# Sorted edge rows placed so that the four rows a partition gets of a unit lie side by side, in a graph network on one core

## The reference

```python
edge_index = jnp.stack([src, dst])        # 206250 edges, sorted by dst, 6250 nodes
x = _layernorm(x + _L0_gnn_ref(x, edge_index, ...))
x = _layernorm(x + _L1_gnn_ref(x, edge_index, edge_attr_64, ...))

# _L0: two layers of   agg = segment_mean(h[src], dst);  relu(agg @ W_l + b_l + h @ W_r)
# _L1:
row, col = (edge_index[0], edge_index[1])
out = jnp.concatenate([x[row], edge_attr], axis=1)
out = jax.nn.selu(out @ W1a + b1a) @ W1b + b1b
summed = jax.ops.segment_sum(out, col, num_segments=x.shape[0])
mean = summed / jnp.maximum(counts, 1.0)[:, None]
h = jnp.concatenate([x, mean, u[batch]], axis=1)
return jax.nn.selu(h @ W2a + b2a) @ W2b + b2b
```

## Time and profile before

| | |
|---|---|
| median of 3 runs | 3544.66 us (3544.01 to 3555.59) |
| the profiled execution | 3541.63 us, span of its instructions 3539.9 us |
| busy share of the span | PE 67%, PEld 48%, DVE 44%, ACT 28%, POOL 51% |
| mean granted TensorE clock | 0.782 of full |
| DMA traffic | 346.58 MB in 478137 packets, 357799 of them under 512 bytes |

### The profile page before, as it was taken

The page is one execution under the profiler, slowest core; times in us unless marked ns, Lnnn a source line. Parts: engine busy times, 40 slices in busy tenths (PEclk is TensorE's granted clock), DMA queues, the critical chain, the costliest instruction groups (busy, mean ns, idle before and its releaser), DMA issues.

```text
span 3539.9 us, 52139 instructions
## 1 busy us (share of the span) xinstructions
PE 2367.1 (67%) x18396; PEld 1684.3 (48%) x18396; DVE 1560.6 (44%) x3112; ACT 989.8 (28%) x2190; POOL 1805.8 (51%) x1857
## 2 busy tenths in 40 slices
PE   2799999887888872465666656565665666564554
PEld 1455555444444432354545545454554554453553
DVE  6689999343443332233433333333333333342333
ACT  3567777100000012122222222222222222221222
POOL 6345555454555547445454544455454444545552
PEclk9999999898989975677777777777777767776556
DMA  6467777659555512322222222222222221221111
GB/s 225 154 186 212 211 249 227 177 171 192 174 175 174 175 40 67 79 43 47 46 47 48 47 43 46 46 45 48 46 48 48 45 44 42 47 46 41 42 38 35
DMA packets 478137, 346.58 MB, mean 98 GB/s; under 512 B 357799, under 2 KB 428536, under 8 KB 474219
## 3 DMA queue, kind: packets, MB, share of 16 engines
q1 hardware_dynamic: 367281, 272.49, 26.9%
q0 software_dynamic: 54368, 57.36, 7.1%
q10 hardware_dynamic: 56250, 13.52, 1.9%
HBM read 200.71 MB, written 142.39 MB: 97 GB/s over the span
## 4 chain that ended last, share of the span: by engine, by line
PE 31%; another core or an unknown queue 25%; issue 20%; DVE 13%; ACT 4%; DMA 3%; SPq 2%; POOL 2%; DVEq 1%; ACTq 0%; POOLq 0%
PE agg_ps L1481 6%; DVE arena L1804 5%; PE u_ps L1612 4%; PE cnt_ps L1573 3%; PE u_ps L1608 2%; PE agg_ps L1622 2%; PE cnt_ps L1352 2%; PE agg_ps L1581 1%; PE v_ps L1598 1%; PE t_ps L1565 1%; PE agg_ps L1359 1%; PE agg_ps L1358 1%; DMA overlapping_rows<-A_sb 1%; DVEq L2121 1%
## 5 line engine op out<-in xcount | busy, mean ns | idle before, releaser
L954 POOL DMA_INDIRECT A_sb<-source_terms,src_cur x1176 | 1120.3, 953 | 1047.9 <-ACT src_cur L1160 707.7
L907 POOL DMA_INDIRECT sorted_edges<-pm_row,pm_to x440 | 480.1, 1091 | 332.2 <-DVE pm_to L1913 208.3
L1612 PE MATMUL u_ps<-arena 128*128 128x64 bf16 x3399 | 252.1, 213 | 355.7 <-issue 354.2
L1481 PE MATMUL agg_ps<-A_sb,arena 128*128 128x448 f16 x1911 | 419.3, 369 | 69.2 <-issue 66.5
L1804 DVE TENSOR_TENSOR arena<-iota_code,arena 128x2048 f16<-128x2048 f16 (+1 forms) x392 | 435.6, 1180 | 38.1 <-PE cnt_ps L1352 36.2
L1049 ACT ACTIVATE A_sb<-cnt_ps 128x392 f32 (+1 forms) x784 | 386.2, 497 | 168.8 <-PE cnt_ps L1352 115.0
L1612 PEld LDWEIGHTS u_ps<-arena 128*128 128x128 bf16 x3399 | 198.5, 111 | 411.5 <-issue 403.0
L2123 DVE TENSOR_TENSOR A_sb<-A_sb,agg_ps 65x48 f32 (+1 forms) x290 | 78.0, 269 | 710.4 <-remote 525.2
L1352 PE MATMUL cnt_ps<-arena 128*128 128x98 f16 x3136 | 283.7, 214 | 54.0 <-DVE arena L1804 23.2
L1481 PEld LDWEIGHTS agg_ps<-A_sb,arena 128*128 128x128 bf16 x1911 | 188.8, 101 | 269.9 <-issue 127.6
L1352 PEld LDWEIGHTS cnt_ps<-arena 128*128 128x128 f16 x3136 | 191.1, 101 | 243.4 <-issue 173.6
(11 more groups left out here) (300 smaller groups left out, 3379.9 us busy)
## 6 DMA issues: line engine op xcount, KB each, us to landing
counts_matrix<-A_sb SPq DMA_DIRECT2D x14, 5488.0 KB, 17.2
A_sb<-counts_matrix SPq DMA_DIRECT2D x12, 5488.0 KB
arena<-in_edge_attr_dram SPq DMA_DIRECT2D x96, 256.0 KB
sorted_edges<-zrow SPq DMA_DIRECT2D x11, 1716.0 KB
A_sb<-source_terms,src_cur POOLq DMA_INDIRECT x1176
arena<-sorted_edges SPq DMA_DIRECT2D x143, 128.0 KB
overlapping_rows<-A_sb SPq DMA_DIRECT2D x1, 13056.0 KB, 39.5
A_sb<-in_edge_attr_dram SPq DMA_DIRECT2D x50, 256.0 KB
```

Source lines behind the costliest of these rows:

```text
L907: pool.indirect_dma_start(out=sorted_d, out_offset=bass.IndirectOffsetOnAxis(ap=pm_to[:, k, j:j + 1], axis=0), in_=pm_row[:, k, j, :], in_ ...
L954: pool.indirect_dma_start(out=gath[k][:, j * F:(j + 1) * F], out_offset=None, in_=p_d, in_offset=bass.IndirectOffsetOnAxis(ap=src_cur[k][: ...
L1481: ins = pe.matmul(agg_ps[:, 0:SBN], Hsb[:, part, blk, :], Asb(half)[:, blk, :], start=False, stop=(part == 2), skip_group_check=True)
L1612: ins = pe.matmul(u_ps[:, j * F:(j + 1) * F], lane_p[u % 2][:, a, j * P:(j + 1) * P], P3[:, 2 * b + a, part, :], start=False, stop=(part = ...
```

## The change

A row's place in `sorted_d` is changed inside its unit. Before, the row with place 128 t + p of a unit (tile t, partition p) lay at 128 t + p; now it lies at 4 p + t. The four rows of a partition are then one piece of 1056 bytes. `slot_group` works out the new number with five more small DVE operations. `load_unit` is one transfer of 128 pieces into `rows_p`. `turn_unit` becomes 4 transposes of 66 columns, one per tile, so that row 64 of `t2_ps` holds the lanes of all 512 edges; `move_unit` copies 64x512 and 1x512; `spread_lanes` is one product of a single row (`pick` row of ones) with 512 columns; `unit_product` does the attribute part tile by tile, with 64 rows of contraction and the 64x64 weights. The ring of `attrT_p` has 2 buffers in place of 3.

```diff
@@ buffers
-        endsT = [edge_buf(P // 2, 2 * UT).bitcast(BF16) for _ in range(2)]
+        endsT = [edge_buf(UT * P // 2, F + 1).bitcast(BF16)[F:F + 1, :] for _ in range(2)]
+        attrT_p = [edge_buf(UT * P, F)]
...
-        attr_p = [edge_buf1(UT * F) for _ in range(UNIT_RING)]
-        ends_p = [edge_buf1(2 * UT) for _ in range(UNIT_RING)]
-        attrT_p = [edge_buf1(UT * F) for _ in range(UNIT_RING)]
+        rows_p = [edge_buf1(UT * (F + 2)).rearrange("p (j f) -> p j f", j=UT) for _ in range(UNIT_RING)]
...
-        pick = sb("pick", [2 * UT, UT, P], BF16)
+        pick = sb("pick", [F + 1, P], BF16)
@@ load_unit
-                sp.dma_start(attr_p[k].rearrange("p (j f) -> p j f", f=F), rows_u[:, :, 0:F]).then_inc(unit_in[k], 16)
-                sp.dma_start(ends_p[k].rearrange("p (j a) -> p j a", a=2), rows_u[:, :, F:F + 2]).then_inc(unit_in[k], 16)
+                sp.dma_start(rows_p[k].rearrange("p j f -> p (j f)"),
+                             sorted_d[u * UT * P:(u + 1) * UT * P, :].rearrange("(p j) f -> p (j f)", p=P)).then_inc(unit_in[k], 16)
@@ move_unit
-                if u >= UNIT_RING:
-                    act.wait_ge(unit_z, UNIT_Z + u - UNIT_RING + 1)
                 if u >= 2:
+                    act.wait_ge(unit_z, UNIT_Z + u - 1)
                     act.wait_ge(lanes_spread, LANES_SPREAD + u - 1)
-                act.activation(attrT_p[u % UNIT_RING], t2_ps[:, 0:UT * F], ACT.Copy)
-                act.activation(endsT[u % 2], t2_ps[0:2 * UT, UT * F:UT * F + P], ACT.Copy).then_inc(unit_moved, 1)
+                act.activation(attrT_p[u % 2], t2_ps[0:F, :], ACT.Copy)
+                act.activation(endsT[u % 2], t2_ps[F:F + 1, :], ACT.Copy).then_inc(unit_moved, 1)
@@ turn_unit
-                for c in range(UT // 2):
-                    pe.transpose(t2_ps[:, c * P:(c + 1) * P], attr_p[k][:, c * P:(c + 1) * P], ident[:, :])
-                pe.transpose(t2_ps[0:2 * UT, UT * F:UT * F + P], ends_p[k], ident[:, :]).then_inc(unit_turned, 1)
+                for j in range(UT):
+                    ins = pe.transpose(t2_ps[0:F + 2, j * P:(j + 1) * P], rows_p[k][:, j, :], ident[:, :])
+                ins.then_inc(unit_turned, 1)
@@ spread_lanes
-                for j in range(UT):
-                    ins = pe.matmul(v_ps[:, j * P:(j + 1) * P], pick[:, j, :], endsT[u % 2], start=True, stop=True)
-                ins.then_inc(lanes_spread, 1)
+                pe.matmul(v_ps[:, :], pick[F:F + 1, :], endsT[u % 2], start=True, stop=True).then_inc(lanes_spread, 1)
@@ unit_product
-                    c = j // 2
-                    if j % 2 == 0:
-                        pe.matmul(u_ps[:, c * P:(c + 1) * P], attrT_p[u % UNIT_RING][:, c * P:(c + 1) * P], Wedge[:, :], start=True, stop=False, skip_group_check=True)
+                    pe.matmul(u_ps[:, j * F:(j + 1) * F], attrT_p[u % 2][:, j * P:(j + 1) * P], Wedge[0:F, 0:F], start=True, stop=False, skip_group_check=True)
@@ slot_group
-                dve.scalar_tensor_tensor(pm_to[:, k, :], pm_rank[:, :], -1.0, pm_else[:, :], ALU.add, ALU.add).then_inc(pm_rows, 1)
+                step(dve.scalar_tensor_tensor(pm_place[:, :], pm_rank[:, :], -1.0, pm_else[:, :], ALU.add, ALU.add))
+                dve.tensor_scalar(pm_lane[:, :], pm_place[:, :], P - 1, None, ALU.bitwise_and).then_inc(dve0, 1)
+                n0[0] += 1
+                step(dve.tensor_scalar(pm_tile[:, :], pm_place[:, :], 7, None, ALU.arith_shift_right))
+                step(dve.tensor_scalar(pm_tile[:, :], pm_tile[:, :], UT - 1, None, ALU.bitwise_and))
+                step(dve.scalar_tensor_tensor(pm_part[:, :], pm_lane[:, :], float(UT - 1), pm_place[:, :], ALU.mult, ALU.add))
+                dve.scalar_tensor_tensor(pm_to[:, k, :], pm_tile[:, :], -float(P - 1), pm_part[:, :], ALU.mult, ALU.add).then_inc(pm_rows, 1)
```

More of the change, by code:

```diff
@@ L328, in build @@
         at1[0] = p_at
-        attr_p = [edge_buf1(UT * F) for _ in range(UNIT_RING)]
-        ends_p = [edge_buf1(2 * UT) for _ in range(UNIT_RING)]
-        attrT_p = [edge_buf1(UT * F) for _ in range(UNIT_RING)]
+        rows_p = [edge_buf1(UT * (F + 2)).rearrange("p (j f) -> p j f", j=UT) for _ in range(UNIT_RING)]
         lane_p = [edge_buf1(2 * UT * P // 2).bitcast(BF16).rearrange("p (a n) -> p a n", a=2) for _ in range(2)]
         hot_p = [edge_buf1(UT * PWIN).rearrange("p (j n) -> p j n", j=UT)]
+        attrT_p.append(edge_buf1(UT * P, F))
+        at1[0] = max(at1[0], p_at + SRC_BLOCKS * F)
         iota_p = edge_buf1(PWIN)
@@ L353, in build @@
         pm_to = sb("pm_to", [P, PRING, EJ], I32)
+        pm_place, pm_lane, pm_tile, pm_part = (sb(n, [P, EJ], I32) for n in ("pm_place", "pm_lane", "pm_tile", "pm_part"))
         pm_seen = sb("pm_seen", [P, 2, NCELL], FP16)
@@ L743, in load_unit @@
             def load_unit(u):
-                k, rows_u = u % UNIT_RING, sorted_d[u * UT * P:(u + 1) * UT * P, :].rearrange("(j p) f -> p j f", p=P)
+                k = u % UNIT_RING
                 if u >= UNIT_RING:
                     sp.wait_ge(lanes_hot, LANES_HOT + u - UNIT_RING + 1)
-                sp.dma_start(attr_p[k].rearrange("p (j f) -> p j f", f=F), rows_u[:, :, 0:F]).then_inc(unit_in[k], 16)
-                sp.dma_start(ends_p[k].rearrange("p (j a) -> p j a", a=2), rows_u[:, :, F:F + 2]).then_inc(unit_in[k], 16)
+                sp.dma_start(rows_p[k].rearrange("p j f -> p (j f)"),
+                             sorted_d[u * UT * P:(u + 1) * UT * P, :].rearrange("(p j) f -> p (j f)", p=P)).then_inc(unit_in[k], 16)
             te = gE * EG
@@ L884, in _ @@
             pool.memset(pm_keep[:, :, :], 1.0).then_inc(pm_const, 1)
-            pool.memset(pick[:, :, :], 0.0).then_inc(pm_const, 1)
+            pool.memset(pick[:, :], 1.0).then_inc(pm_const, 1)
             pool.wait_ge(pm_const, PM_CONST + 4)
@@ L889, in _ @@
             pool.memset(pm_keep[:, :, 0:1], 0.0).then_inc(pm_const, 1)
-            pool.affine_select(out=pick[:, :, :], in_=pick[:, :, :], compare_op=ALU.not_equal, fill=1.0,
-                               base=0, pattern=[[-2, UT], [0, P]], channel_multiplier=1).then_inc(pm_const, 1)
             pool.iota(lane_col[:, :], [[P, 2]], 0, 1, allow_small_or_imprecise_dtypes=True).then_inc(pm_const, 1)
@@ L1585, in turn_unit @@
                 k = u % UNIT_RING
-                pe.wait_ge(unit_in[k], UNIT_IN[k] + 32 * (u // UNIT_RING + 1))
+                pe.wait_ge(unit_in[k], UNIT_IN[k] + 16 * (u // UNIT_RING + 1))
                 if u >= 1:
                     pe.wait_ge(unit_moved, UNIT_MOVED + u)
-                for c in range(UT // 2):
-                    pe.transpose(t2_ps[:, c * P:(c + 1) * P], attr_p[k][:, c * P:(c + 1) * P], ident[:, :])
-                pe.transpose(t2_ps[0:2 * UT, UT * F:UT * F + P], ends_p[k], ident[:, :]).then_inc(unit_turned, 1)
+                for j in range(UT):
+                    ins = pe.transpose(t2_ps[0:F + 2, j * P:(j + 1) * P], rows_p[k][:, j, :], ident[:, :])
+                ins.then_inc(unit_turned, 1)
             def spread_lanes(u):
@@ L1921, in _ @@
             dve.wait_ge(pm_dst_in, PM_DST_IN + 16)
-            dve.wait_ge(pm_const, PM_CONST + 9 + sum(len(cell_runs(t)) for t in CELL_TILES))
+            dve.wait_ge(pm_const, PM_CONST + 8 + sum(len(cell_runs(t)) for t in CELL_TILES))
             step(dve.tensor_scalar(pm_below[:, :], pm_dst[:, :], -1.0, None, ALU.add))
@@ L2138, in make_lanes @@
                 dve.tensor_tensor(hot_p[u % 2], agg_ps[:, PWIN:2 * PWIN].unsqueeze(1).to_broadcast([P, UT, PWIN]),
-                                  ends_p[u % UNIT_RING].rearrange("p (j a) -> p j a", a=2)[:, :, 1].unsqueeze(2).to_broadcast([P, UT, PWIN]), ALU.is_equal)
+                                  rows_p[u % UNIT_RING][:, :, F + 1].unsqueeze(2).to_broadcast([P, UT, PWIN]), ALU.is_equal)
                 dve.tensor_scalar(lane_p[u % 2][:, 0, :], v_ps[:, :], lane_col[:, 0:1], None, ALU.is_equal)
```

## The result

The changed kernel takes 3625.06 us (median of 4 runs, 3612.41 to 3627.38) against 3544.34 before (4 runs): 1.0201 times, interval 1.0174 to 1.0228. Measured again beside other kernels, in five rounds, it was 1.0141 times before (1.0108 to 1.0175). So it is slower by 1.4 to 2.0%; 3622 was forecast. In microseconds the first measurement has 81 more, and the second, on a before of 3519, 50 (38 to 62); the forecast growth was 77.

The account below looks back on a forecast made before the run. Edge stage taken as bound by POOL's gather bursts plus gaps waiting for indices, stage 1 by DVE, stage 2 by PE. Terms 64 + 11 + 2 = 77 us on 3544.66 gave 3622 us; 8-in-10 range 3538 to 3685.

Parts of the forecast that it names:

- 13 and 64: Forecast growth: 11 us in stage 1 plus 2 in stage 2, and 64 us (31 to 88) for the edge stage's units.
- The sign on POOL's wait for `src_cur`: Edge stage: POOL's total wait for the indices should be 40 to 90 us above 628.3, in about 84 waits.
- DVE's operations: Five small slot_group operations, 0.20 us apart: +11 us in stage 1 (0 to 16), where DVE is the bound.
- The 2 us for stage 2: Stage 2: +2 us for steps where DVE's work for PE is queued behind a slot_group; 44 us if uncovered.
- ACT's copies: Edge stage: two 512-element copies lengthen a gap by 0.56 to 0.80 us, 0.56 taken; ACT last in 56 of 84 gaps.
- the dear product: Attribute product as eight narrow records on PE, at the dear price: +0.79 us, possibly in 28 gaps where DVE is last.
- ACT's close row: Middle gap: move_attr, two copies, selu and indices without idle time between copies and selu, read as ACT being last.
- the dear end of 0.20: Upper price of a narrow attribute-product record on PE, about 0.20 us as line 1573's; the low price was 0.086.
- the 0.20 that the sum had: turn_unit on PE: four transposes for three, +0.20 us ahead of the copies.
- The light load: Rival: fewer packets of unit loads relieve gathers or waits, making the kernel faster, 3490 to 3534 us; chance 0.18.
- Hidden growth: Rival: transposes and copies fall into slack in the gaps, leaving only stage 1's growth, 3551 us; chance 0.08.
- PE as the bound: Rival: dear narrow products cost 1.2 us in each of 112 slots, 134 us, giving 3692 us; chance 0.06.

Follow-up runs that it names:

- the second trace: The changed kernel itself, nothing altered, traced again beside the last experiments; measured there at 1.0141 times the kernel before.
- the three parts together: The kernel before with the five DVE operations, four narrow attribute products (128 rows of contraction) and two 512-element copies; 1.0148 times before.
- the run with the old packets: The changed kernel with a unit loaded again in two transfers, 512 pieces of 256 bytes and 512 of 8; 1.0148 times before, 3605 us.
- the copies' run: The kernel before with both move_unit copies 512 elements long per partition, on two buffers; 1.0118 times before.
- ACT's late copies: move_unit of a slot's last step put behind the next slot's indices on ACT: 0.9877 on the kernel before, 1.0060 on the changed kernel.

## Why the prediction came out

**Where the time went.** 16.7 us ahead of the first gather and 67 us behind it, against 13 and 64. The side and the size were right, and the range held. Yet that forecast and result lie 3 us apart is luck: the terms were not all of the right size, and the second measurement has 50 us where 77 were forecast. The sign on POOL's wait for `src_cur`, 40 to 90 us above 628.3, did not come: the totals are 639.2 and 650.0, since a fixed stretch holds fewer slots when each takes longer.

**DVE's operations.** 11 us for stage 1 was right: 11 by the means of fourteen traces. The 2 us for stage 2 do not show in them. The spacing of 0.20 us holds where nothing disturbs; the tail at 344 us has operations of 1.03 and 0.53 us, and before's had one of 0.49, so not all of it is new. What the ratio of the operations alone, 26 us (17 to 35), holds beyond the 11 stays open. That PE does not use what `slot_group` makes is not so by the program: in `layer2` it waits for the count that `pm_to` raises. In the changed kernel's trace that wait came last twice, for 0.9 us in all, in before's never.

**ACT's copies.** The mechanism is shown: longer copies alone cost 1.2%, and copies out of the way of the indices make both kernels faster. The growth was 0.77 us per pair and not 0.56. I took the short spacing that the pair had shown before; the row of the same length, 0.62 us, was the right one, and it stood in the range.

**PE.** This is the mis-sized term. "If the dear product lies on the way to DVE as well, 0.79 more" put it in 28 gaps, and half of it in the sum. Alone it costs 64 to 75 us, where 11 stood for it in the sum. The growth of busy time in a unit step is 0.88 us (282.5 against 168.2 us over the stretch; 0.77 by the second trace), and 84 gaps of it are 74 us, so the size fits PE on the way in about all gaps; gap by gap this was not followed. ACT's close row was read as ACT being last; but ACT's row begins with a wait of 1.73 us for PE's transposes, which stand behind the product. Both are on one way there, one after the other, and that idle time belongs to the question of what is ahead of a step, not only what is in front of the selu. The price of a record was taken from the wrong row: line 1573's 0.20 us, while the product's own row has 168.2 us over 568, 0.30 each. The narrow record takes 0.26 us (0.27 with 128 rows), above the dear end of 0.20; both sides were priced too low, and their difference, 0.88 for 0.79, came out near. The depth of contraction hardly changed the load (233 ns for 248) or the time (64 us for 75). The transposes were dearer in count but hardly in time: the four of 66 columns take 114.1 us, where three took 67.8 and 45.2, which is 0.03 us more a unit (0.11 in the second trace) for the 0.20 that the sum had.

**Why the sum still came out.** The parts' costs overlap: 4.0% alone, 1.5% together. The term for the product was too small (by the ratio alone also that for DVE's operations) and the overlap was left out, and these cancel. How they overlap is not shown. One reading is that a product that ends later moves PE's waits on issue and so shares them with other delays; these are 351.8 us before, 240.3 with the narrow product alone and 208.1 in the changed kernel, but 316.3 with the three parts together, which does not fit it. Of the changed kernel's own two ratios, 0.6% apart, some may lie between chips. This stays open.

**The rivals.** The light load is out by the run with the old packets. Whether the queue's small share or the early issue is the reason, no run tells. "Hidden growth" is out by the copies' run. PE as the bound, which I gave 0.06 at 1.2 us in every slot, was nearer in its place, every gap, and wrong in its sum.

## What to carry to other kernels

Read for each gap not only what stands next to the step that ends it, but the whole way from the last thing that was free; an idle time at the head of a close row puts the engine behind it on the way too. Costs of parts that lie in the same wait are not to be added without a run of them together, and a wait that vanishes from the list is no gain by itself. Where a slow queue (here POOL's gathers) is paced by an index, try what is not needed for the index behind it in its engine's program: here that gave 1.2% on ACT, while the like move on PE, of the spread, lost 3.3%.

## What the runs showed of the hardware

In the kernel before, PE's bf16 products with full loads stand at "issue", in gaps of up to 2.6 us: 351.8 us over 396 waits, of which 247 us lie wholly inside POOL's bursts of indirect transfers. With plain transfers of the same 128 pieces of 256 bytes there are none, the record's mean falls from 212 to 193 ns, and the kernel falls from 3528 to 2348 us (one execution). The granted clock in the edge stage goes from 0.73 to 0.98 of full, that is from a mean between its two levels of 1.2 and 2.4 GHz to nearly always the higher one, with PE busy 94% of the stretch in place of 62%. Yet indirect transfers in flight are not enough: in the changed kernel with ACT's late copies 911 gathers go on in the stretch and the same products wait 3.7 us in all, after PE has stood 357.1 us for the copies ahead of them. By what way an indirect transfer holds PE up, and why not there, no run here tells.

A transpose's time did not go by its count: a group of four with 66 columns took 0.83 us of busy time a unit (0.90 in the second trace), three of 128, 128 and 8 took 0.80. A copy on ACT from PSUM takes 0.59 us for 512 elements, whether 1, 64 or 128 partitions take part.
